# A chain of attention and expert layers: K/V projected two units later, the last join moved into the tail, LayerNorm of outputs moved to the end, row statistics at stage ends

## The reference

```python
x = x + L0_xattn(layernorm(x), ctx, mask, ...)   # cross-attention, 16 heads of 32, 2048 keys per batch, with a mask
x = x + L0_attn(layernorm(x), ...)               # retention, 16 query heads, decay, causal
x = x + L0_ffn(layernorm(x), ...)                # 8 experts, the best 2 per row, hidden size 2048
x = x + L1_xattn(layernorm(x), ctx, ...)         # cross-attention without a mask; LayerNorm of its output
x = x + L1_attn(layernorm(x), ...)               # RWKV-like: mixing with the row before, a scan, a gate
x = x + L1_ffn(layernorm(x), ...)                # 8 experts, the best 2 per row, gate and up projections
```

```python
q = split_heads(Q @ Wq.T + bq); k = split_heads(K @ Wk.T + bk); v = split_heads(V @ Wv.T + bv)
probs = softmax(where(mask, q @ k.T / sqrt(32), -1e9))      # the second one has no mask
out = (probs @ v) @ Wo.T + bo                               # the second one: LayerNorm(out) * gamma + beta
```

## Time and profile before

| | |
|---|---|
| median of 3 runs | 2318.66 us (2317.45 to 2320.69) |
| profiled execution | 2317.28 us, its span 2315.5 us |
| PE busy | 2114.3 us (91%), 14761 instructions |
| DVE busy | 1419.9 us (61%) |
| ACT busy | 1362.7 us (59%) |
| POOL busy | 299.8 us (13%) |
| TensorE's clock, mean granted | 0.964 of full |

### The profile page before, as it was taken

One profiled execution on the slowest core, in us unless ns is written; L12 is line 12 of the kernel. 1 busy time (PEld: TensorE's weight loads), 2 busy tenths in 40 slices (PEclk: granted clock), 3 DMA queues, 4 the chain that ended last, 5 costly groups with the idle time before them and its releaser, 6 DMA issues. The chain is left out here.

```text
span 2315.5 us, 37828 instructions
## 1 busy us (share of the span) xinstructions
PE 2114.3 (91%) x14761; PEld 1633.6 (71%) x14761; DVE 1419.9 (61%) x2392; ACT 1362.7 (59%) x2595; POOL 299.8 (13%) x270
## 2 busy tenths in 40 slices
PE   6999999999968977799999979999999999866798
PEld 4777777777744545688888746877787777645676
DVE  5455555454544864499999854554554454667687
ACT  2566566566544433488888725666666665541675
POOL 2111112121110000100000221121111120101001
PEclk9999999999988988999999989999999999977999
DMA  4000010101004003599999730010100100022887
GB/s 155 19 23 35 20 38 20 38 19 38 1 1 179 1 1 130 223 386 367 356 358 364 268 141 19 20 38 19 38 20 19 38 20 19 2 73 105 325 336 265
DMA packets 53585, 262.34 MB, mean 113 GB/s; under 512 B 9496, under 2 KB 9880, under 8 KB 26528
## 3 DMA queue, kind: packets, MB, share of 16 engines
q1 hardware_dynamic: 47104, 244.71, 28.2%
q0 software_dynamic: 2560, 8.39, 1.1%
q10 hardware_dynamic: 3744, 6.82, 0.8%
HBM read 243.91 MB, written 15.99 MB: 112 GB/s over the span
## 5 line engine op out<-in xcount | busy, mean ns | idle before, releaser
L512 DVE COPY c_pt<-bank 128x512 f32<-128x512 f32 x256 | 177.0, 691 | 549.3 <-PE bank L341 549.2
L664 ACT ACTIVATE c_pr<-wide,c_nmax 128x512 f32<-128x512 f32 x512 | 349.3, 697 | 164.8 <-DVE c_nmax L504 83.8
L231 POOL TENSOR_TENSOR c_clo<-c_raw,c_chi 128x512 fp32r<-128x512 f32 x122 | 158.2, 1299 | 1012.1 <-ACT c_chi L641 1012.1
L341 PE MATMUL bank<-ident,c_pr 128*128 128x128 f32 x2048 | 268.7, 273 | 14.0 <-DVE c_pt L512 11.8
L341 PEld LDWEIGHTS bank<-ident,c_pr 128*128 128x128 f32 x2048 | 238.0, 140 | 49.9 <-DVE c_pt L512 14.0
L649 ACT ACTIVATE c_khi<-bank,c_cols 128x512 fp32r<-128x512 f32 x128 | 88.1, 688 | 252.2 <-PE bank L94 252.2
L92 PE MATMUL bank<-c_wv_hi,c_chi 128*128 128x512 f32 x512 | 218.2, 426 | 15.7 <-DVE c_clo L442 14.4
L1664 DVE TENSOR_TENSOR moe_wlo<-moe_raw,moe_whi 128x2048 fp32r<-128x2048 f32 x97 | 219.1, 2284 | 17.2 <-ACT moe_whi L1520 17.2
L92 PE MATMUL bank<-c_chi,c_wk_hi 128*128 128x512 f32 x512 | 213.7, 417 | 8.8 <-ACT c_v L655 8.7
L94 PE MATMUL bank<-c_wv_hi,c_clo 128*128 128x512 f32 x512 | 202.8, 396 | 0.0
L93 PE MATMUL bank<-c_wv_lo,c_chi 128*128 128x512 f32 x512 | 202.7, 396 | 0.0
(11 more groups left out here) (371 smaller groups left out, 4044.4 us busy)
## 6 DMA issues: line engine op xcount, KB each, us to landing
moe_hr<-in_L_ffn_w SPq DMA_DIRECT2D x68, 1024.0 KB, 7.0
moe_raw<-in_L_ffn_w SPq DMA_DIRECT2D x52, 1024.0 KB, 7.0
c_raw<-in_ctx SPq DMA_DIRECT2D x32, 1024.0 KB, 4.9
moe_raw<-in_L_ffn_we_gate SPq DMA_DIRECT2D x15, 1024.0 KB, 7.0
moe_raw<-in_L_ffn_we_up SPq DMA_DIRECT2D x15, 1024.0 KB, 6.6
moe_raw<-in_L_ffn_we_down SPq DMA_DIRECT2D x15, 1024.0 KB, 6.6
slot_outputs<-moe_ob ACTq DMA_DIRECT2D x26, 256.0 KB, 6.0
ret_w<-in_L_attn_w_attn SPq DMA_DIRECT2D x4, 1024.0 KB, 9.2
```

The source lines that it names most:

```text
L231: nc.gpsimd.tensor_tensor(clo[:, g % 2, c, :], raw[:, c, :], f32(chi[:, g % 2, c, :]), ALU.subtract) \
L341: last = pe.transpose(TB[n % 2][:, h * P:(h + 1) * P], pr[:, u % 2, h, n * P:(n + 1) * P], k["ident"][:])
L512: nc.vector.tensor_copy(pt[:, n, :], TB[0][:]).then_inc(pt_dve, 1)
L664: nc.scalar.activation(pr[:, u % 2, h, :], S[h][:], ACT.Exp, bias=nmax[:, b % 2, i, at:at + 1], scale=-1.0 if masked else 1.0, accum_out=d ...
```

## The change

Both cross-attentions:
- K/V are projected two units ahead of the scores instead of four (`LAG = 2`): two units of chunk 0 before the loop, the others inside it, so units 0 to 61 project and 62 and 63 don't. `project_q(2)` and `(3)` move into unit 0; q goes into the banks `QB`; `scores(0)` waits for the first two parts of q only.
- Wv and the first raw chunk are loaded, cast and cut in halves; the first products start with the first piece. POOL no longer makes the first low part. `turn_x` uses four banks, and `keep_xT` is shared by ACT and DVE.
- Batch 2 is closed at u = 62 and 63 instead of 51 and 52.
- The last join: POOL scales `acc` and the early half of `part` (heads 0 to 7) and adds them; for the last two units DVE scales the block straight out of PSUM and adds it (`join_block`). `turn_last(0)` and `(1)` turn the halves, `project_out(3)` follows each piece of `aT`.
- In the second one, `measure_out` keeps every batch's rows in a place of their own, and the root, the scaling and the adding to x (`scale_out`) come at the end: for three batches together, then for the last.

All stages: the statistics of x's rows (`measure_rows`) are computed at the end of the stage before, into tiles that outlive it, and `root_table` has ACT load the table of the root at a stage's end. Only the first stage still measures x itself.

```diff
+def measure_rows(nc, s, k, x, b):
+    s.then(nc.vector.bn_stats(k["stats"][:, b, :], x[:, b, :]))
+    s.then(nc.vector.bn_aggr(k["mv"][:, b, :], k["stats"][:, b, :]))
+    s.mark(nc.vector.tensor_scalar_add(k["ve"][:, 0, b:b + 1], k["mv"][:, b, 1:2], LN_EPS))
+    s.mark(nc.vector.tensor_scalar(k["ve"][:, 1, b:b + 1], k["mv"][:, b, 1:2], 1.0 + LN_EPS, LN_EPS * LN_EPS, ALU.mult, ALU.add))
+
+def root_table(nc, k):
+    nc.scalar.sqrt(k["root"][:], k["ones"][:, 0:1])
...
-    LAST = U + (7 if norm else 5)
+    LAG = 2
+    TURN = {PER + 3: 0, 2 * PER + 3: 1, U - 2: 2}
+    OUT = {u + 1: b for u, b in TURN.items()}
...
+        QB = (S[2], S[3], OB, TB[1])
...
-                sp.dma_start(wv_raw, t[L + "Wv"]).then_inc(wv_in, 16)
-                sp.dma_start(raw[:].rearrange("p c n -> p (c n)"), t["ctx_1024"][0]).then_inc(raw_in, 16)
+                for i in range(2):
+                    part_of = slice(i * HALF, (i + 1) * HALF)
+                    sp.dma_start(wv_raw[:, part_of], t[L + "Wv"][:, part_of]).then_inc(wv_in[i], 16)
+                    sp.dma_start(raw[:].rearrange("p c n -> p (c n)")[:, part_of], t["ctx_1024"][0][:, part_of]).then_inc(first_in[i], 16)
...
+                mine, new = acc[:, (NB - 1) % 2, :], part[:, (NCH - 1) % 2, :]
+                early = HEADS // 2
+                pool.wait_ge(joined, 3 * NB - 1)
+                pool.wait_ge(wn_done, NB)
+                nc.gpsimd.tensor_tensor(by_heads(mine, HEADS), by_heads(mine, HEADS),
+                                        wn[:, 0, :].unsqueeze(2).to_broadcast([P, HEADS, HD]), ALU.mult).then_inc(acc_scaled, 1)
+                pool.wait_ge(oc_done, U - 2)
...
                     pe.wait_ge(klo_done, C * g + o + 1)
-                    if u == 0:
-                        pe.wait_ge(q_done, C)
+                    if u < C:
+                        pe.wait_ge(q_done, max(u + 1, 2))
...
                 project_v(0, 0)
+                project_v(0, 1)
                 project_k(0, 0)
-                project_v(0, 1)
+                if x_in is not None:
+                    turn_x()
                 project_k(0, 1)
...
                 project_q(0)
-                project_k(0, 2)
                 project_q(1)
-                project_v(0, 3)
-                project_q(2)
-                project_k(0, 3)
-                project_q(3)
-                for u in range(LAST):
-                    g, o = u // C, u % C
-                    ahead = g + 1 < G
-                    closing = u >= PER + 3 and (u - 3) % PER == 0
+                for u in range(U + 2):
+                    g, o = (u + C - LAG) // C, (u + C - LAG) % C
+                    ahead = g < G
                     if u < U:
                         scores(u)
+                    if u == 0:
+                        project_q(2)
                     if 2 <= u < U + 2:
                         outputs(u - 2)
                     if ahead:
-                        project_v(g + 1, o)
+                        project_v(g, o)
+                    if u == 0:
+                        project_q(3)
...
+                def join_block(u):
+                    o = u % C
+                    mine, new = (rows[:, o * P:(o + 1) * P] for rows in (acc[:, (NB - 1) % 2, :], part[:, (NCH - 1) % 2, :]))
+                    dve.wait_ge(wn_done, NB)
+                    dve.wait_ge(o_turned, u + 1)
+                    nc.vector.tensor_tensor(new.rearrange("p (h d) -> p h d", h=HPT), OB[:, P:2 * P].rearrange("p (h d) -> p h d", h=HPT),
+                                            wn[:, 1, o * HPT:(o + 1) * HPT].unsqueeze(2).to_broadcast([P, HPT, HD]), ALU.mult).then_inc(oc_done, 1)
+                    dve.wait_ge(oc_done, u + 1)
+                    dve.wait_ge(acc_scaled, 1)
+                    nc.vector.tensor_tensor(mine, mine, new, ALU.add).then_inc(late_joined, 1)
...
+                if norm:
+                    scale_out(0, NB - 1)
+                    dve.wait_ge(done, NB - 1)
+                else:
+                    dve.wait_ge(out_read, NB - 1)
+                for b in range(NB - 1):
+                    measure_rows(nc, s, k, x, b)
+                finish(NB - 1)
+                if norm:
+                    measure_out(NB - 1)
+                    s.wait()
+                    scale_out(NB - 1, 1)
+                    dve.wait_ge(done, NB)
+                else:
+                    dve.wait_ge(out_read, NB)
+                measure_rows(nc, s, k, x, NB - 1)
```

In retention the rows 0 to 2 are measured before the last `add_output` and row 3 after it; in the first expert layer and in rwkv each row is measured right after its last addition:

```diff
                     nc.vector.tensor_tensor(x[:, b, :], x[:, b, :], ps[b][:], ALU.add).then_inc(s_["out"], 1)
+                    if first:
+                        dve.wait_ge(s_["out"], b + 1)
+                        measure_rows(nc, s, k, x, b)
...
-                for b in range(NB):
-                    s.mark(nc.vector.bn_stats(stats[:, b, :], x[:, b, :]))
-                s.wait()
-                for b in range(NB):
-                    s.mark(nc.vector.bn_aggr(mv[:, b, :], stats[:, b, :]))
-                s.wait()
```

More of the change, by code:

```diff
@@ L574, in _, with scale_out @@
-                if x_in is None:
+                    s.mark(nc.vector.scalar_tensor_tensor(out=y[b], in0=y[b], scalar=mv[:, b, 0:1], in1=gamma_row,
+                                                          op0=ALU.subtract, op1=ALU.mult))
+                def scale_out(first, n):
+                    dve.wait_ge(ystd, 1 if first == 0 else 2)
+                    s.then(nc.vector.reciprocal(rstd[:, first:first + n], std[:, first:first + n]))
+                    for b in range(first, first + n):
+                        nc.vector.scalar_tensor_tensor(out=x[:, b, :], in0=y[b], scalar=rstd[:, b:b + 1], in1=x[:, b, :],
+                                                       op0=ALU.mult, op1=ALU.add).then_inc(done, 1)
```

359 lines of the change are left out of this document (202 added, 157 removed).

## The result

The changed kernel took 2299.7 us (median, 2299.0 to 2300.2) against 2318.7 for the kernel before: ratio 0.9912, 95% interval 0.9900 to 0.9924. It is faster by 19 us, not by the 39.6 of the forecast, and it lies outside the stated range of 2264 to 2295. Its profiled execution took 2300.2 us with a span of 2298.5, 17.0 less than the span before; the sum had 39.6, so 22.6 us are to be explained.

The account below looks back on a forecast made before the run. The prediction took PE, busy 91% of the span, as the bound, so only its work or idle time counted. Terms of -39.6 took 2317.28 to 2277.7, and 1.4 for the median gave 2279 us, range 2264 to 2295.

Parts of the forecast that it names:

- the sum: Whole kernel: all terms for heads, batch 2, last joins, LayerNorm and statistics added up, -39.6 us.
- The loop: Cross-attention loops: units of 9.5 us up to u = 61; lost slack of klo costs 0.
- LayerNorm out of the loop: Second cross-attention: without ACT's table changes after closings, three pairs of units each save 3.0 us, -9.0.
- The tails: Cross-attention ends, last join inside the tail: 13.0 instead of 20.8 us (-7.8) and 20.1 instead of 24.6 (-4.5).
- (b): Rival: early statistics pay at every stage start too, 3.0 us at four, giving 2267; chance 0.12.
- (c): Rival: later K/V make project_v wait for DVE in every unit, 86 us over 124 units, giving 2365; chance 0.05.
- (d): Rival: joins, closings, LayerNorm, statistics and heads fail to gain as planned, 40 us lost, giving 2319; chance 0.03.
- the term for rows 2: Closing batch 2 in both cross-attention tails: loop saves 5.7 us, net -1.8 each, -3.6.
- the first head: First cross-attention's start: scores(0) at 36.9 us, scores(2) at 60.9 instead of 77.85, -17.0.
- Rival (a): Heads: gaps keep PE's clock low through unit 0, 6.5 us a head, giving 2292; chance 0.14.
- the second head: Second cross-attention's start: scores(2) 53.5 us after the first DMA's issue instead of 71.7, -18.2.
- The statistics: Row statistics at stage ends: retention +1.2, first expert layer +2.8, rwkv +4.8, second expert layer -3.1; together +5.7 us.

Follow-up runs that it names:

- e8: Changed kernel with the block of rows 2 closed in the loop again (units 51 and 52) instead of units 62 and 63: 2302.0 us.
- E1: Changed kernel with GpSimd's four low parts and four bias additions in both heads held until two, respectively all four, queries are kept: 2292.1 us.
- E2: Changed kernel with ScalarE's wait for bias columns moved behind keep_v, and column bv on its own semaphore: 2294.0 us.
- e9: Kernel of e6 with TensorE reordered: v(0,2) before scores(0) in the first head, queries between keys in the second: 2271.7 us.
- e7: Changed kernel with Wv and the first chunk each loaded in one whole transfer, casts still in halves: 2298.8 us.
- e4: Changed kernel with the root of the first three blocks' variances taken at unit 64, ahead of the second cross-attention's last join: 2293.7 us.
- e12: Changed kernel with TensorE's transposes at the first expert layer's start held until the first router weight has landed: 2298.6 us.
- e3: Changed kernel with row statistics back at the stages' starts and no root table loaded at stage ends: 2286.6 us.
- e6: Changed kernel with four edits together: statistics back at starts, GpSimd's operations behind the queries, column wait moved, root early: 2280.0 us.
- e10: Changed kernel with the first expert layer's four casts and cuts of xT put ahead of the first router weight: 2294.7 us.
- e5: The changed kernel run again without any edit, as the measure for the single edits: 2297.3 us.

## Why the prediction was wrong

**Right.** The loop: units of 9.5 up to u = 61 apart from the two closings, and from unit 2 on no wait on `klo` in it (PE 584.0 of 589.7 us busy from scores(2) to 663; in unit 1 it waits 0.66 once). LayerNorm out of the loop: no pair of 11 is left. The tails, with the waits of PE at 0.55 and 0.78 and the last 8 products in 3.61 us; before they had 5.64 and 5.43. Timelines and stretches of after:
```profile
679.70 0.44 PE L432 MATMUL bank<-ident,c_acc 128*128 128x128 f32 x2 [0.55 <-POOL c_acc L305]
...
681.03 0.44 PE L432 MATMUL bank<-ident,c_acc 128*128 128x128 f32 x2 [0.78 <-DVE c_acc L599]
681.30 3.61 PE L442 MATMUL bank<-c_woT,c_aT 128*128 128x512 f32 x8
...
673.73:686.90 13.17, 8.82 (x95) 5.41 (x94) 9.29 (x32) 4.56 (x11) 2.34 (x3) 1.00 0.00 1
2004.80:2025.09 20.29, 8.82 (x95) 5.41 (x94) 15.65 (x46) 4.76 (x12) 2.35 (x3) 0.87 0.00 0
```
13.2 and 20.3 us against the forecast's 13.0 and 20.1 (the earlier trace rows had 20.8 and 24.6). Rwkv's end cost 4.8, its rows 2.5 us apart, as said. Rivals (b), (c) and (d) did not occur. Right in its direction and too small was the term for rows 2: some 3.5 us a stage instead of 1.8 (e8). As the stretch from scores(2) to the first stage's end shrank by 2.6 and the sum had 2.2, its other terms there gave 1.3 less; unit 62, where PE waits 2.94 us for DVE and is slow behind it, is the place that shows, and no run takes it apart.

**Wrong: the first head, 12.4 of the 22.6 us.** It failed at four steps of the layout; their prices overlap, and scores(0) alone varies by 2.4 us between profiles of the same code. (1) "`keep_q(1)` makes PE wait 3.0, as 3.13 now": the wait was 8.0. It was taken over from a row in which POOL was idle beside it; the change moves POOL's eight operations onto `keep_q(0)`. E1: 5.1 us. I had asked what POOL's adds would meet, but only in the second stage, and only for one of two queries. (2) "from first statistic to last `xn` it takes 5.49 us: 22.0": it took 7.6, as the root stood on ACT behind `keep_v`, and that behind a column's landing. The row came from a stage in which ACT had nothing else to do. E2: 3.2 us (1.9 to 4.3) with what PE's clock gave back. (3) Two `project_q` of 3.1: they take 3.56 each (7.13 for 16 instructions in e9), 1.8 us for the four. (4) The weights' landing behind the halves: by e7 at least 2.2 us, part of which is (2), since the column comes earlier too. Rival (a), the low clock through unit 0, was half true: unit 0 took 16.6 instead of 14.6 at a mean clock of 0.80, and in e9, without the long wait, 10.7 at 1.00 (with 2.8 us of its work moved ahead). Its price of 8.3 is a slip for what it names: 3.5 and 24 times 0.23 make 9.0; with the 0.43 us from start to start that slow products take in the trace, 0.20 more each, it is 8.3.

**Wrong: the second head, 4.9.** "By the same steps" was the step that failed. In the first head `turn_x` stands between the two keys and covers the way of `klo(0,0)` to the free bank; in the second it stands at the beginning, and PE waits 1.7 us there, 3.3 for the query (e1: 2.2 without POOL) and 0.8 for the cut of Wk. E9 took 3.4 out by order alone. And the first half of Wv was cast 4.8 us after its issue, as late as a whole one (4.9 before and in e7), 4.1 to 4.8 over the profiles with halves; in the first stage it was 4.0, where the forecast had 3.5.

**The statistics, 5.2 by the first profile.** Each had its sign right. The second expert layer came out 1.9 short of the sum, and this is no step of the forecast that failed: its transposes start 3.1 us earlier (3.0 instead of 6.1 after the stage's start, as forecast) and the first expert's products 3.3, and in seven of the nine profiles with this code the stage took 201.7 to 202.3 us, 2.7 to 3.3 less than before; the first profile (203.8) and e4 (205.1) are the exceptions. Retention and the first expert layer came out 3.2 over the sum. The first expert layer's first product came 0.5 later, its clock came back later and the first scatter came 1.3 later; this appears in the runs with late statistics and also in one with early ones (e9), so it stays open whether the change has a part in it (e12 excludes one way). The same holds for retention's first row (100.9 against 100.1, 100.0 in e3 and 100.8 in e6). That four starts would save nothing against the kernel before was right, and for the first expert layer e10 shows why: both engines stood at the weight's transfer with work for which x was ready.

## What to carry to other kernels

When an edit shortens one engine's way, write down what the other engines do in the new time slots: a duration read beside an idle GpSimd doesn't hold for an operation between SBUF tiles beside a busy one, and moving GpSimd's work by a semaphore cost nothing here (e1). In a head, put the wait that lands last behind everything that doesn't need it, on each queue, for columns and weights alike, and look for PE's waits at chains that end in one bank. Statistics moved to a stage's end stand on the path wherever VectorE ends the stage (in full in rwkv, 4.8 us); in this kernel they paid only where the next stage had something to do with x before its first transfer landed. And take the same code's stage from several profiles before you explain 2 us of it: unit 0, unit 62 and the second expert layer each had two lengths here.

## What the runs showed of the hardware

- A GpSimd subtraction or addition between SBUF tiles slows DVE's beside it by a lot: four multiplications of 128x128 took 4.52 us instead of 0.90, a cast of 128x512 1.37 instead of 0.43, a subtraction 1.63 instead of 0.69. GpSimd's own four operations took 4.99 and 5.24 us beside them, 4.96 and 5.03 without them (e1).
- Two transfers of 512 KB in place of one of 1 MB, twice in a row, delayed what came behind them: Wk's cast started at 13.75 instead of 12.89 (13.6 to 14.1 in all profiles with halves), the column's landing ended a wait at 20.72 instead of 19.03.
- The same code had its clock back at different points: unit 0 of the first stage took 14.9 (e3), 15.1 (e4), 16.4 (e5) and 16.6 us (the first profile). The Trainium skill (TensorE: Matmul & The Clock Gate, What's actually happening) says that the number of slow products of one kernel varies from run to run; the traces agree, with 1.7 us here.
- A table load took 1.28 us, and the activation stands 0.02 behind it (21.81 to 23.09, 23.11); no drain shows between them. Moved into a gap it cost nothing (e4).
